# Sixteen-head attention with its eight head pairs written out, and a gated feed-forward whose chunks are prepared at other places

## The reference

```python
x = x + tanh(g_xattn[0]) * perceiver_attention(ctx, mask, layernorm(x))   # 16 heads of 64; keys: 1601 context rows and the 2048 tokens
x = x + tanh(g_ffn[0])   * lora_ffn(layernorm(x))
x = x + tanh(g_xattn[1]) * cross_attention(layernorm(x), ctx)             # 16 heads of 16
x = x + tanh(g_ffn[1])   * local_transformer(layernorm(x))                # 2 layers
```

```python
h = shift_token(x)                    # the upper 128 channels come from the token before
h = (h - mean(h)) / sqrt(var(h) + 1e-5) * lg + lb
a, g = split(h @ w1 + b1, 2)          # 682 hidden channels each
x = x + (a * gelu(g)) @ w2 + b2
```

## Time and profile before

| | us |
|---|---|
| median of 3 runs | 3603.16 (3602.57 to 3606.04) |
| profiled execution, its own time | 3604.71 |
| span in the trace | 3602.6 |
| 16-head attention, first to last pair step | about 110 to 1950 |
| gated feed-forward, layer 0 and layer 1 | about 2959 to 3127 and 3437 to 3593 |
| busy in the span: PE, DVE, ACT, POOL | 3216.9, 2208.4, 1949.8, 159.7 |
| mean granted clock of PE | 0.95 |

### The profile page before, as it was taken

How to read it: one execution, slowest core, us unless ns; L and a number is a source line. 1 busy time by engine, 2 the same in 40 slices (tenths; PEclk the granted TensorE clock), 3 DMA queues, 4 the chain that set the end, 5 groups by cost and what they waited for, 6 DMA issues and landing times. The chain is left out here.

```text
span 3602.6 us, 72202 instructions
## 1 busy us (share of the span) xinstructions
PE 3216.9 (89%) x28528; PEld 1680.6 (47%) x28528; DVE 2208.4 (61%) x2722; ACT 1949.8 (54%) x2413; POOL 159.7 (4%) x189
## 2 busy tenths in 40 slices
PE   3999999999999999999997886999959978699868
PEld 2544444343443433444454761112227756567656
DVE  5677777767787777777787560000157645466545
ACT  3555555645556556555564135999816742167521
POOL 0000000000000000000000102000011110011110
PEclk8999999999999999999999798999979988899989
DMA  1000000000000000000000011111010000100000
GB/s 47 7 2 6 3 2 8 1 7 3 2 6 3 6 4 2 6 3 2 3 2 28 1 59 43 31 27 28 16 51 1 1 30 1 51 1 1 1 30 24
DMA packets 23622, 49.58 MB, mean 14 GB/s; under 512 B 5679, under 2 KB 16514, under 8 KB 22146
## 3 DMA queue, kind: packets, MB, share of 16 engines
q1 hardware_dynamic: 23298, 44.97, 3.8%
HBM read 39.10 MB, written 5.83 MB: 12 GB/s over the span
## 5 line engine op out<-in xcount | busy, mean ns | idle before, releaser
L625 ACT ACTIVATE a_probs<-PS 128x1024 f32<-128x1024 f32 x928 | 949.6, 1024 | 657.5 <-PE PS L463 650.6
L476 PE MATMUL PS<-a_probs,a_V 64*64 64x512 f32 x7424 | 968.0, 589 | 5.3 <-DVE a_heads_outT L679 5.3
L712 DVE TENSOR_TENSOR a_prob_sums<-a_prob_sums,a_probs 128x1024 f32<-128x1024 f32 x512 | 627.3, 1225 | 201.2 <-ACT a_probs L625 196.9
L709 DVE SCALAR_TENSOR_TENSOR a_prob_sums<-a_probs,a_valid,a_prob_sums 128x1024 f32<-128x1024 f32 x384 | 482.9, 1258 | 75.8 <-ACT a_probs L625 65.8
L1274 ACT ACTIVATE c_probs<-PS 128x1024 f32<-128x1024 f32 (+1 forms) x416 | 380.7, 1115 | 42.6 <-PE PS L1217 39.6
L463 PE MATMUL PS<-a_Q_hi,a_K_hi 64*64 64x512 f16 x3712 | 382.8, 386 | 0.0
L463 PE MATMUL PS<-a_Q_hi,a_K_lo 64*64 64x512 f16 x3712 | 377.2, 379 | 0.2 <-issue 0.2
L463 PE MATMUL PS<-a_Q_lo,a_K_hi 64*64 64x512 f16 x3712 | 377.0, 379 | 0.0
L476 PEld LDWEIGHTS PS<-a_probs,a_V 64*64 64x64 f32 x7424 | 278.8, 133 | 171.6 <-issue 19.2
L463 PEld LDWEIGHTS PS<-a_Q_hi,a_K_hi 64*64 64x64 f16 x3712 | 112.8, 106 | 301.7 <-issue 291.5
L1227 PE MATMUL PS<-c_probs,c_Vh 128*32 128x512 f32 (+1 forms) x1664 | 224.8, 613 | 6.0 <-ACT c_probs L1274 5.2
(11 more groups left out here) (301 smaller groups left out, 4141.4 us busy)
## 6 DMA issues: line engine op xcount, KB each, us to landing
c_Qop<-q_part SPq DMA_DIRECT2D x96, 64.0 KB, 2.2
c_Kop<-k_part SPq DMA_DIRECT2D x96, 50.0 KB, 2.0
d_tables<-in_rotary_dram SPq DMA_DIRECT2D x2, 1792.0 KB, 11.3
d_wqkv<-in_l1f_wqkv_dram SPq DMA_DIRECT2D x2, 1536.0 KB, 7.5
f_w<-in_l1f_w_dram SPq DMA_DIRECT2D x2, 1536.0 KB, 5.8
X<-in_x_dram SPq DMA_DIRECT2D x1, 2048.0 KB, 8.1
out_dram<-X SPq DMA_DIRECT2D x4, 512.0 KB, 3.6
c_cT<-in_ctxT_dram SPq DMA_DIRECT2D x1, 1601.0 KB, 6.6
```

Of the source, the lines that this page charges most:

```text
L476: last = nc.tensor.matmul(m.PS[64 * h:64 * h + 64, PVB + g, :], V[e][rows, s, 64 * h:64 * h + 64], probs[n % 4][rows, h * BANK:(h + 1) * B ...
L625: nc.scalar.activation(probs[n % 4][:], m.PS[:, b0:b0 + 2, :].rearrange("p b c -> p (b c)"), ACT.Exp).then_inc(exped, 1)
L709: nc.vector.scalar_tensor_tensor(out=sums, in0=new, scalar=valid[:, s:s + 1], in1=sums, op0=ALU.mult, op1=ALU.add).then_inc(summed, 1)
L712: nc.vector.tensor_tensor(sums, sums, new, ALU.add).then_inc(summed, 1)
```

## The change

Two edits. First, the loop over pairs is replaced by eight calls, on PE, ScalarE and DVE. Second, in the feed-forward the steps that prepare a chunk are put at other places on all four engines:

- chunk 1 is shifted right behind chunk 0, at the start, into its own PSUM bank (5), and its statistics, root and staging come in the start-up too; its turn stays where it was;
- chunks 2 and 3 are shifted before the lower of two chunks earlier and turned behind that lower; ScalarE's and DVE's steps for them stand there too.

```diff
@@ context_attention
         def pairs(engine, pair):
-            pair(0, 0, True, False)
-            with engine.Fori(0, PAIRS // 2 - 1) as j:
-                pair(j * 2 + 1, 1, False, False)
-                pair(j * 2 + 2, 0, False, False)
-            pair(PAIRS - 1, 1, False, True)
+            for i in range(PAIRS):
+                pair(i, i % 2, i == 0, i == PAIRS - 1)
@@ shifted_ffn
-SHIFT_BANK, H_BANK, DOWN_BANK = 6, 6, 4
+SHIFT_BANKS, H_BANK, DOWN_BANK = (6, 5, 6, 6), 6, 4
@@ shifted_ffn, POOL
                 copy_first_half(0)
+                copy_first_half(1)
                 pool.wait_ge(s["w1_hi"], l + 1)
                 for t in range(GT):
                     take_lo(nc.gpsimd, w1_lo[:, :, :, t, :], w1[:, :, :, t, :], w1_hi[:, :, :, t, :]).then_inc(s["w1_split"], 1)
-                copy_first_half(1)
@@ shifted_ffn, PE
                 def shift_half(c):
-                    after(pe, "h_moved", base + c)
+                    if c > 1:
+                        after(pe, "h_moved", base + c)
...
                 shift_half(0)
+                shift_half(1)
                 turn_h(0)
                 raise_tiles(0, range(LEAD))
                 for c in range(CH):
-                    if c + 1 < CH:
-                        shift_half(c + 1)
                     raise_tiles(c, range(LEAD, GT - 2))
-                    if c + 1 < CH:
-                        turn_h(c + 1)
+                    if c == 0:
+                        turn_h(1)
                     raise_tiles(c, range(GT - 2, GT))
                     if c + 1 < CH:
                         raise_tiles(c + 1, range(LEAD))
+                    if c + 2 < CH:
+                        shift_half(c + 2)
                     lower(c)
+                    if c + 2 < CH:
+                        turn_h(c + 2)
@@ shifted_ffn, ScalarE
                 move_shifted(0)
+                move_shifted(1)
                 root(0)
                 act.wait_ge(s["w1_in"], 48 * (l + 1))
                 move_h(0)
+                root(1)
                 for t in range(LEAD):
                     gelu(0, t)
                 for c in range(CH):
-                    if c + 1 < CH:
-                        move_shifted(c + 1)
-                        root(c + 1)
                     for t in range(LEAD, GT - 2):
                         gelu(c, t)
-                    if c + 1 < CH:
-                        move_h(c + 1)
+                    if c == 0:
+                        move_h(1)
                     for t in range(GT - 2, GT):
                         gelu(c, t)
                     if c + 1 < CH:
                         for t in range(LEAD):
                             gelu(c + 1, t)
+                    if c + 2 < CH:
+                        move_shifted(c + 2)
+                        root(c + 2)
+                        move_h(c + 2)
@@ shifted_ffn, DVE
                 split_h(0)
+                statistics(1)
+                stage(1)
                 for t in range(LEAD):
                     gate(0, t)
                 for c in range(CH):
-                    if c + 1 < CH:
-                        statistics(c + 1)
-                    for t in range(LEAD, GT - 3):
+                    for t in range(LEAD, GT - 2):
                         gate(c, t)
-                    if c + 1 < CH:
-                        stage(c + 1)
-                    gate(c, GT - 3)
                     if c + 1 < CH:
                         split_h(c + 1)
...
                         for t in range(LEAD):
                             gate(c + 1, t)
+                    if c + 2 < CH:
+                        statistics(c + 2)
+                        stage(c + 2)
                     output(c)
```

More of the change, by code:

```diff
@@ L1791, in shift_half @@
                 def shift_half(c):
-                    after(pe, "h_moved", base + c)
-                    nc.tensor.matmul(m.PS[:, SHIFT_BANK, :], shift[:, 0, :], Z[:, 4 * c:4 * c + 4, P:D],
+                    if c > 1:
+                        after(pe, "h_moved", base + c)
+                    nc.tensor.matmul(m.PS[:, SHIFT_BANKS[c], :], shift[:, 0, :], Z[:, 4 * c:4 * c + 4, P:D],
                                      start=True, stop=False)
                     first = 1 if c == 0 else 0
-                    nc.tensor.matmul(m.PS[:, SHIFT_BANK, first * P:BANK], shift[:, 1, :],
+                    nc.tensor.matmul(m.PS[:, SHIFT_BANKS[c], first * P:BANK], shift[:, 1, :],
                                      Z[:, 4 * c + first - 1:4 * c + 3, P:D], start=False, stop=True).then_inc(s["shifted"], 1)
@@ L1855, in move_shifted @@
                     act.wait_ge(s["shifted"], base + c + 1)
-                    nc.scalar.activation(shifted[c % 2][:, :, P:D], m.PS[:, SHIFT_BANK, :].rearrange("p (j n) -> p j n", n=P),
+                    nc.scalar.activation(shifted[c % 2][:, :, P:D], m.PS[:, SHIFT_BANKS[c], :].rearrange("p (j n) -> p j n", n=P),
                                          ACT.Copy).then_inc(s["shift_moved"], 1)
```

## The result

| | us |
|---|---|
| before, median of 4 runs on the same chip | 3602.89 (3602.57 to 3606.04) |
| changed kernel, median of 4 runs | 3564.93 (3559.63 to 3571.88) |
| ratio, 95% interval | 0.9894 (0.9879 to 0.9909) |
| difference | -38.0 |
| profiled execution of the changed kernel, its own time; span | 3571.88; 3570.1 |

The forecast was 3558, in a range of 3548 to 3572. The profiled execution is the slowest of the four, so its trace shows less of the gain (32.8 us against 3604.71) than the medians do. In this trace nearly all of it is the feed-forward's: the two layers are 16.3 and 16.5 us shorter, the pair stage (first score to last product with V) takes 1837.2 us where it took 1837.8.

A forecast was written before the change was run, and what follows sets the result against it. PE was taken as the bound, busy 3216.9 of 3602.6 us, so its waits count. From 3604.7, part A's 10 and part B's 35.4 give 3559.3; the median 1.5 lower makes 3558, range 3548 to 3572.

The forecast's parts named there:

- Part A: Pair stage: writing out the pairs makes the two back-edge borders like the other five; gain 10 us, range 4 to 16.
- Gaps inside pairs: Pair stage: PE idle time inside a pair, named as a sign that the prediction is wrong; no size given.
- rival 3: Pair stage: written-out text must be fetched, three 3.3 us fetches in each of six pairs, 59 us; time 3617; chance 0.03.
- The mean of 4.2 us for a border: Pair stage: mean cost, idle plus slow clock, of the five borders without a back edge, taken for the other two.
- Part B: Feed-forward: preparing chunks earlier removes three gaps (9.8 us), shift (1.7) and slow clock (6.2); 17.7 us per layer, 35.4 for two.
- The covers: Feed-forward: time left before PE would wait on moved steps: 1.1 us at start-up, 3.1 beside lower, 1.4 before tile 4.
- Upper bound: Feed-forward: gain of at most 35.4 us over two layers, since start-up and the last tile's tail stay.
- the lower bound: Feed-forward: 11.5 us per layer, 23 for two, if the clock drops all the same at other places.
- the signs that it named: Borders 2.5 to 4.3 us idle, pairs busy 230 to 231.6, full clock to the last lower, layers 17 to 18 us shorter.
- Rival 1: Pair borders: the guard takes all, part A is worth nothing; time 3568; chance 0.08.
- What sets a guard branch at 3.3 or 4.7 no row tells: Head of every pair: guard branch stays, its cost unexplained; part A left open from loss 0.5 to gain 22 us.
- nothing is kept for reuse: Instruction fetch: the Trainium skill's statement, by which rival 3 is impossible and the guards stay dear at 3.3 to 4.7 us.

The follow-up runs named there:

- the pairs alone: The eight pairs written out on the kernel before, feed-forward left as before: 3596.72 us, ratio 0.9976.
- the two halves tried alone: On the kernel before, loop kept: only chunk 1 prepared in the start-up, 3586.34 us; only chunks 2 and 3 shifted ahead of the lower before them, 3581.61 us.
- the two layers of 137.2 us: Layer 1 of two variants of the changed kernel: PE's guard condition turned round (3566.94 us); guarded form replaced by one small matmul (3532.90 us).
- the condition turned round: Changed kernel with PE's unguarded form first, head branch not taken, and a jump over the guarded form at the pair's end: 3566.94 us, ratio 0.9908.
- the last kernel: Changed kernel with PE's guarded forms of all pairs behind the last pair, and VectorE keeping the bound as a running maximum: 3534.86 us, ratio 0.9815.

## Why the prediction was right

**Part A** (forecast 10 us, measured 6.9, interval 4 to 13, which holds the forecast). The mechanism held: without the back edge all seven borders are alike, 2.6 to 2.9 us idle in the changed kernel, and none takes 7. That is even less than the mean of the five straight borders in the earlier trace rows. Two terms were left out. First, idle time inside the pairs: 4.1 us in the profile of the changed kernel, 3.9 in that of the pairs alone, two thirds of it the stop at the start of pair 7. "Gaps inside pairs" stood among the signs that would prove the prediction wrong; they came, only much smaller than rival 3 needed (it decided from some 60 us). Second, the clock. The mean of 4.2 us for a border took a slow clock behind three of five; in the changed kernel it came behind six of seven, after idle times of 2.6 to 2.9 us. What decides that was not found: in the earlier trace rows borders of 2.5 and 2.9 us had none. So 10 came near partly by luck: in the one traced execution of the changed kernel the stop in pair 7 and the slow clock took back nearly all of what the borders gave (0.6 us left in the stage), in that of the pairs alone 5.7 us were left.

**Part B** (forecast 35.4 us, measured 31.4, interval 27 to 39). Each term that was to go has gone: three gaps of 3.28, the shift, and the slow stretches behind the gaps; the two halves tried alone give 6.7 and 9.6 us a layer, by terms 6.6 and 11.1. The covers of 1.1 us (start-up), 3.1 (beside the lower) and 1.4 (table load before tile 4) held: no such matmul waits. The term that was missing stands against "Upper bound: the same 35.4, since the start-up and the last tile's tail stay". The tail stayed, 2.08 us idle, but not its clock: the slow stretch behind it, 3.4 us at half, costs 1.7 us a layer, and 17.7 - 1.7 = 16.0 against the measured 16.3 and 16.5. That is the mechanism of the lower bound ("the clock drops all the same at other places"), at one place of three. It isn't there in every execution: the two layers of 137.2 us gained 18.9, and there the start-up's slow stretch was shorter as well. So the upper bound was no bound either.

**The sum.** 6.9 + 31.4 = 38.3 against 45.4 forecast; the forecast's time was 7 us low, within its range. Of the signs that it named, those of the clock and what hangs on them failed: pairs busy up to 232.6 us and not 231.6, no full clock up to the last lower, layers shorter by 16.3 and 16.5 us and not by 17 to 18. **Rival 1** (the guard takes all, A worth nothing) is excluded by the pairs alone, whose interval doesn't reach 1. **Rival 3** had the wrong size and the right subject: text is fetched, and PE does sometimes wait for it, 4 us in all. Its premise is wrong for this loop: nothing of the body was kept, since 47, 47 and 46 transfers of instructions (16 KB each) came in during its three iterations.

**What the prediction passed by.** It kept the guard at 3.3 to 4.7 us as a fixed price: "What sets a guard branch at 3.3 or 4.7 no row tells". Rows of the kernel before did tell. The cross attention has a guard of the same kind on PE (L1241), always taken, over the same text of 192 matmul calls each time. It is passed eight times: in the first head pair, then in a loop whose back edge is L1261. Its first two passes, its other six, and the loop's branch:

```profile
L1241 PEldq COMPARE_BRANCH  x2: 3322/3596/3870, 2173.5 to 2249.7; - x2
...
L1241 PEldq COMPARE_BRANCH  x6: 208/208/223, 2303.8 to 2549.1; - x6
...
L1261 PEldq COMPARE_BRANCH  x7: 76/208/227, 2303.3 to 2597.9; - x7
```

One branch over one distance costs 3.3 us the first time that the loop's text is run and 0.2 from then on, and the back edge 0.2 us from the start. From 2303.5 to 2597 us not one of the 16 KB transfers comes in: this loop, with 320 matmuls in a pass, runs on text that is already there. The pair loop, with 5110 in an iteration, is transferred anew each time. So what counts is whether the target has been fetched, and distance counts through that. Seen in time, this would have shown that the guards' price could be avoided and that eight of them, and not the two back edges, were the larger sum in the pair stage: the far jumps that remain in the changed kernel are worth 30 us, the two that the change removed 7. It also corrects the prediction's "nothing is kept for reuse": the text of this short loop is, and the measurement decides.

## What to carry to other kernels

Look for the branches that are carried out over long text before looking at loops: on PE a fall-through branch costs 0.06 to 0.09 us here, a jump to text that is there 0.2 to 0.4, one to text that has yet to be fetched 3.3 to 5 and often a slow clock behind it. A loop short enough to be kept paid only 0.2 us a branch after its first pass, so look at the long ones. Put the rare form at the end of the stage and let the common one fall through; where a loop forbids this, writing it out is worth more for that than for its back edge. And when gaps go from a stage, add the clock behind the gaps that stay to the sum: one that was free before may be charged now.

## What the runs showed of the hardware

- On PE a jump's price goes by whether its target has been fetched, not by being taken: 208 to 361 ns over one matmul, 3.3 to 5.0 us over a pair's text, 64 to 89 ns if not taken; over the same text 3322 ns in a loop's first pass and 208 to 223 in later ones. Putting it at the end of the body changes nothing. On ScalarE and VectorE the records of the pair loop's back edge are short (45 and 63 ns), but behind the first of them the next instruction starts only 2.6 and 2.8 us later. The Trainium skill (Runtime: NRT & Kernel Launch, Instruction fetch mechanics) says that a taken branch outside of what has been fetched stalls; the runs agree (3.3 to 5.0 us), and show that one inside it costs 0.2 to 0.4 us.
- A far jump can stop PE twice: 2.4 to 2.7 us idle, some matmuls, then 2.2 to 3.0 us more, in which one transfer of instructions (16 KB) lands. It is seen behind both back edges without a guard, and behind pair 7's guard in the changed kernel and in that with the pairs alone, but not in that with the condition turned round. In the changed kernel a second transfer begins 3.0 to 3.6 us after the first behind all seven guards, and PE runs out only at pair 7. That the target there lies near the end of its piece of text would explain it; this was not tried.
- Straight text is not free either: stops of 0.1 to 0.9 us in the middle of dense matmuls, eleven in the written-out kernel without a guard, two in pairs 1 to 6 of the last kernel, none in pairs 1 to 6 of the kernel before. They end 2.2 to 2.9 us after a transfer of instructions began. Why most transfers cause none, and why that changes with the layout, stays open.
- The granted clock can fall to 0.50 for 3.4 us behind an idle time of only 2.1 us. It did in ten of the twelve layers in which the clock had been 1.00 for long before (some 99 us in the changed kernel), and in none of the ten layers whose last slow stretch had ended some 30 us earlier. In the two exceptions the clock had been 1.00 for some 99 us as well, so the time at full clock alone does not decide it; what does stays open.
